# Key projection ahead of the head loop, in seven block products, with the result kept in DRAM

## What is computed

```python
x = _rmsnorm(hidden_states, ln_weight)
h_q = (x @ w_q.T).reshape(b, lq, H, DH)
h_k = (key_value_states @ w_k.T).reshape(b, lk, H, DH)
h_v = (key_value_states @ w_v.T).reshape(b, lk, H, DH)
score = jnp.einsum('bqhd,bkhd->bhqk', h_q, h_k) + position_bias[None]
# masked softmax over k
attn = jnp.einsum('bhqk,bkhd->bqhd', score, h_v).reshape(b, lq, H * DH)
return hidden_states + attn @ w_out.T
```

## Time and profile before

| what | value |
|---|---|
| median of 3 runs (lowest, highest) | 1074.19 us (1074.11, 1076.26) |
| the profiled execution, first to last instruction | 1071.4 us |
| first `turn_probs` of the loop | 73.04 us |
| last `turn_probs` but one | 903.27 us |
| busy: PE, DVE, ACT, POOL | 97%, 62%, 43%, 29% |
| bytes moved by DMA | 52.39 MB, 49 GB/s on the mean |

### The profile page before, as it was taken

The page is one execution under the profiler, slowest core; times in us unless marked ns, Lnnn a source line. Parts: engine busy times, 40 slices in busy tenths (PEclk is TensorE's granted clock), DMA queues, the critical chain, the costliest instruction groups (busy, mean ns, idle before and its releaser), DMA issues.

```text
span 1071.4 us, 16826 instructions
## 1 busy us (share of the span) xinstructions
PE 1037.1 (97%) x5946; PEld 903.5 (84%) x5946; DVE 659.0 (62%) x1189; ACT 458.9 (43%) x1090; POOL 313.4 (29%) x236
## 2 busy tenths in 40 slices
PE   8989999999999999999999999999999999799995
PEld 7778888888888888888888888888888888578784
DVE  5766666666666666666666666666666666853615
ACT  6866343434343434343434343434343434254251
POOL 1645040404040404040404040404040402343204
PEclk9999999999999999999999999999999999899998
DMA  9402020202020202020202020202020300300011
GB/s 299 134 1 84 2 84 1 83 0 83 0 83 0 83 0 83 0 83 0 83 0 83 0 83 0 83 0 83 0 83 0 122 1 20 109 21 1 1 40 40
DMA packets 20698, 52.39 MB, mean 49 GB/s; under 512 B 3136, under 2 KB 7232, under 8 KB 20672
## 3 DMA queue, kind: packets, MB, share of 16 engines
q1 hardware_dynamic: 20672, 52.06, 14.6%
HBM read 49.95 MB, written 2.10 MB: 49 GB/s over the span
## 4 chain that ended last, share of the span: by engine, by line
PE 88%; DVE 5%; POOL 2%; ACT 2%; issue 1%; DMA 1%; DVEq 0%; SPq 0%; POOLq 0%; ACTq 0%
PE psum L1330 25%; PE psum L1332 25%; PE psum L1331 25%; PE psum L1336 8%; PE psum L1337 3%; PE psum L1463 3%; DMA raw<-in_dft 1%; POOL rows L511 1%; DVE st L1045 0%; PE psum L1568 0%; DVE wts L1012 0%; POOL stat L581 0%; DVE rsum L1240 0%; ACT xn_hi L647 0%; POOL stat L583 0%
## 5 line engine op out<-in xcount | busy, mean ns | idle before, releaser
L539 POOL TENSOR_TENSOR smx<-far,bias 128x512 f32<-128x512 f32 x64 | 82.7, 1292 | 423.2 <-DVE smx L1068 421.5
L735 ACT ACTIVATE smx<-smx,nmax 128x128 f32<-128x128 f32 x256 | 99.8, 391 | 231.8 <-DVE nmax L1074 231.8
L976 DVE TENSOR_TENSOR qk<-psum,qk 128x512 fp32r<-128x512 f32 x136 | 93.2, 687 | 105.1 <-ACT qk L647 105.1
L1330 PE MATMUL psum<-wv_lo,cx_hi 128*128 128x256 f32 x512 | 149.7, 292 | 0.3 <-DVE xn_lo L976 0.3
L1332 PE MATMUL psum<-wv_hi,cx_hi 128*128 128x256 f32 x512 | 144.5, 282 | 0.0
L1331 PE MATMUL psum<-wv_hi,cx_lo 128*128 128x256 f32 x512 | 144.5, 282 | 0.0
L647 ACT ACTIVATE qk<-psum 128x512 fp32r<-128x512 f32 x136 | 80.8, 596 | 140.7 <-PE psum L1332 140.6
L976 DVE TENSOR_TENSOR vv_lo<-psum,vv_hi 128x512 fp32r<-128x512 f32 x64 | 44.2, 691 | 124.9 <-ACT vv_hi L647 124.9
L489 POOL TENSOR_TENSOR wqk_lo<-raw,wqk_hi 128x1024 fp32r<-128x1024 f32 x31 | 74.3, 2396 | 127.8 <-ACT wqk_hi L647 127.8
L1330 PE MATMUL psum<-wo_lo,at_hi 128*128 128x512 f32 x256 | 105.9, 414 | 1.1 <-issue 1.1
L1330 PE MATMUL psum<-cx_lo,wqk_hi 128*128 128x512 f32 x256 | 100.3, 392 | 1.8 <-DVE wqk_lo L976 1.8
(11 more groups left out here) (184 smaller groups left out, 2351.7 us busy)
## 6 DMA issues: line engine op xcount, KB each, us to landing
raw<-in_wqk SPq DMA_DIRECT2D x32, 512.0 KB, 3.4
raw<-in_wv SPq DMA_DIRECT2D x16, 512.0 KB, 4.3
raw<-in_wo SPq DMA_DIRECT2D x16, 512.0 KB, 3.3
raw<-in_ffn SPq DMA_DIRECT2D x10, 512.0 KB, 3.3
raw<-in_dft SPq DMA_DIRECT2D x7, 512.0 KB, 4.6
acc<-in_x SPq DMA_DIRECT2D x2, 1024.0 KB, 9.1
raw<-in_ctxT SPq DMA_DIRECT2D x4, 512.0 KB, 10.2
bias<-in_bias SPq DMA_DIRECT2D x32, 64.0 KB, 1.8
```

Of the source, the lines that this page charges most:

```text
L539: nc.gpsimd.tensor_tensor(bm, far[:, HB * hf:HB * hf + HB, :], g_, ALU.add).then_inc(s_bm_ready, 1)
L735: a.activation(exps[:, b, :], scores_sb[:, b, :], ACT.Exp, bias=nmax[:, 1, b:b + 1], accum_out=esum[:, 0, b:b + 1]).then_inc(s_exp_done, 1)
L976: return v.tensor_tensor(dst, src, hi, ALU.subtract)
L1330: mm(out, lhs(0), rhs(1), start=first, stop=False)
```

## The change

The K projection leaves the loop. All of K = context x Wk is computed ahead of the loop, pair by pair, in a phase of its own between the second Fourier transform and the first Q projection. For one pair, K is the product of a 256 x 512 matrix of weights and the 512 x 1024 context. It is cut into 2 x 2 blocks and computed by a scheme with seven block products where the plain one has eight, at the price of sums before and after: four sums of context blocks, once (T1 to T4, `t_sums` on DVE), four sums of weight blocks per pair (S1 to S4, `k_sums` and `k_last_sum` on POOL) and seven sums per pair of the products (`k_pair_dve` on DVE, with one copy by ACT, `x_copy`). A block product (`k_product`) is 6 matmuls of 512 columns; the seven of a pair go through banks 0 to 3 in turn. The four resulting blocks of a pair, 256 KB each and one for each unit j, are stored to a DRAM tensor `k_blocks` (`store_block`). In the loop they are loaded back (`load_block`) into `kf`, two to four units ahead, and split into `qk` by ACT (`k_hi`) and POOL (`k_lo`, behind `bias_and_mask`).

The loop's PE order stays, without K: Q(n+1), `turn_probs(n)`, `values(n+2)`, `attend(n)`, `scores(n+1)`, `outputs(n-2)`. `psO[1]` moves from bank 3 to `psT`, bank 2, and `turn_probs(n)` waits until `add_out` has emptied it (`s_o_add` >= 2n - 4); `values` no longer waits for `add_out`.

Also moved: the correlation of the second half (at p = 1) and its delays and norms and all transposes (at p = 5, 7, 9 and 11) go into the K phase; the weights of Q and K come as separate inputs, Q's in one piece a pair; the buffers share SBUF in another way (`av`, `wvq`, `mix`, `kf`, `ssum`, `RING` 1 for 4); the feed-forward weights take other slots, and some of them are split later (after the last unit's exponentials, one by DVE). The diff, cut to its core:

```diff
+        kd = nc.dram_tensor("k_blocks", (4 * PAIRS, P, HALF), F32, kind="Internal").ap()
...
-        psQ, psK, psT, psV = banks[0:4]
-        psO = [psK, psV]
+        psQ, psT, psV = banks[0], banks[2], banks[3]
+        psO = [banks[1], psT]
+
+        def product_bank(p, block):
+            return banks[(BLOCKS * p + block) % 4]
...
+            def store_block(p, i):
+                sp.wait_ge(s_c[i], p + 1)
+                sp.dma_start(kd[4 * p + i], staged[i]).then_inc(s_kst[i], 16)
+
+            def load_block(g, j):
+
+                if is_first(g):
+                    sp.wait_ge(s_kst[j], 16)
+                else:
+                    if isinstance(g, int):
+                        sp.wait_ge(s_k_lo, 4 * g + j - 3)
+                    else:
+                        sp.wait_ge(s_k_lo, 4 * g + (j - 3))
+                    sp.wait_ge(s_kst[j], 16 * PAIRS)
+                sp.dma_start(kf_row(j), row(kd, 4 * g + j)).then_inc(s_kf[j], 16)
...
+                    load_block(g + 1, 0)
+                    sp.wait_ge(s_wq_lo, 2 * g + 2)
+                    load_wq(g + 1)
+                    sp.wait_ge(s_wv_lo, g + 1)
+                    load_wv(g + 1)
+                    load_block(g + 1, 1)
+                load_wo(g)
+                if not last:
+                    load_block(g + 1, 2)
+                    load_bias(g + 1, 0)
+                    load_block(g + 1, 3)
+                    load_bias(g + 1, 1)
...
+            def k_sums(p):
+
+                pc = k_piece(p)
+                pool.wait_ge(s_landed[pc % SLOTS], 16 * (pc // SLOTS + 1))
+                if due(p):
+                    pool.wait_ge(s_ks_vlo, 4 * p - 2)
+                g.tensor_tensor(k_half(p, S3), k_half(p, A11), k_half(p, A21_PLACE), ALU.subtract).then_inc(s_s_sum, 1)
+                pool.wait_ge(s_s_sum, 4 * p + 1)
+                g.tensor_tensor(k_half(p, S1), k_half(p, A21_PLACE), k_half(p, A22), ALU.add).then_inc(s_s_sum, 1)
+                pool.wait_ge(s_s_sum, 4 * p + 2)
+                g.tensor_tensor(k_half(p, S2), k_half(p, S1), k_half(p, A11), ALU.subtract).then_inc(s_s_sum, 1)
+
+            def k_weights_lo(p, block, nth):
+
+                split_lo(s_ks_hi, s_ks_plo, BLOCKS * p + block + 1, k_half(p, block), k_weights(0, block),
+                         k_weights(1, block))
+
+            def k_last_sum(p):
+
+                pool.wait_ge(s_ks_plo, 3 * p + 2)
+                pool.wait_ge(s_s_sum, 4 * p + 3)
+                g.tensor_tensor(k_half(p, S4), k_half(p, A12), k_half(p, S2), ALU.subtract).then_inc(s_s_sum, 1)
+
+            def k_pair_pool(p):
+
+                if p + 1 < PAIRS:
+                    k_sums(p + 1)
+                    k_weights_lo(p + 1, A11, 1)
...
+            def k_lo(n, g_, j):
+                split_lo(s_k_hi, s_k_lo, n + 1, kf_row(j), qk[0][:, 1], qk[1][:, 1])
...
-                    if not (last and j == 3 or is_first(g) and j == 0):
+                    if not (last and j == 3):
                         bias_and_mask(n + 1, *nxt(g, j))
+                        k_lo(n + 1, *nxt(g, j))
...
+            def k_weights_hi(p, block):
+
+                if block in (A11, A12, A22):
+                    pc = k_piece(p)
+                    act.wait_ge(s_landed[pc % SLOTS], 16 * (pc // SLOTS + 1))
+                else:
+                    act.wait_ge(s_s_sum, 4 * p + {S3: 1, S1: 2, S2: 3, S4: 4}[block])
+                if p == 0:
+                    act.wait_ge(s_dft_mm, 4)
+                else:
+                    act.wait_ge(s_kp_mm, BLOCKS * (p - 1) + block + 1)
+                copy_hi(k_weights(0, block), k_half(p, block)).then_inc(s_ks_hi, 1)
+
+            def x_copy(p):
+
+                act.wait_ge(s_kp_mm, BLOCKS * p + 1)
+                if due(p):
+                    act.wait_ge(s_c[C11], p)
+                a.activation(xcopy, product_bank(p, A11), ACT.Copy).then_inc(s_xc, 1)
...
+            def k_hi(n, g, j):
+
+                act.wait_ge(s_kf[j], 16 * (g + 1))
+                if due(n):
+                    act.wait_ge(s_scores_mm, n)
+                copy_hi(qk[0][:, 1], kf_row(j)).then_inc(s_k_hi, 1)
...
+                    if front:
+                        k_hi(n + 1, *nxt(g, j))
...
+            def t_sums(c):
+
+                first, second = raw[:, (DFT_PIECES + 2 * c) % SLOTS], raw[:, (DFT_PIECES + 2 * c + 1) % SLOTS]
+                b11, b12 = first[:, 0:HALF], first[:, HALF:TOK]
+                b21, b22 = second[:, 0:HALF], second[:, HALF:TOK]
+                for i in range(2):
+                    pc = DFT_PIECES + 2 * c + i
+                    dve.wait_ge(s_landed[pc % SLOTS], 16 * (pc // SLOTS + 1))
+                if c:
+                    dve.wait_ge(s_tt_lo, 4 * c)
+                v.tensor_tensor(t_sum(T1), b12, b11, ALU.subtract).then_inc(s_t_sum, 1)
+                dve.wait_ge(s_t_sum, 4 * c + 1)
+                v.tensor_tensor(t_sum(T2), b22, t_sum(T1), ALU.subtract).then_inc(s_t_sum, 1)
+                v.tensor_tensor(t_sum(T3), b22, b12, ALU.subtract).then_inc(s_t_sum, 1)
+                dve.wait_ge(s_t_sum, 4 * c + 2)
+                v.tensor_tensor(t_sum(T4), b21, t_sum(T2), ALU.subtract).then_inc(s_t_sum, 1)
...
+            def k_pair_dve(p):
+
+                front = p + 1 < PAIRS
+                dve.wait_ge(s_xc, p + 1)
+                dve.wait_ge(s_kp_mm, BLOCKS * p + S2 + 1)
+                v.tensor_tensor(u2, product_bank(p, S2), xcopy, ALU.add).then_inc(s_tu2, 1)
...
+                dve.wait_ge(s_tu2, p + 1)
+                v.tensor_tensor(u3, product_bank(p, S3), u2, ALU.add).then_inc(s_tu3, 1)
+                if front:
...
+                dve.wait_ge(s_kp_mm, BLOCKS * p + S1 + 1)
+                dve.wait_ge(s_tu3, p + 1)
+                if due(p):
+                    dve.wait_ge(s_kst[C22], 16 * p)
+                v.tensor_tensor(staged[C22], product_bank(p, S1), u3, ALU.add).then_inc(s_c[C22], 1)
+                if due(p):
+                    dve.wait_ge(s_kst[C12], 16 * p)
+                v.tensor_tensor(staged[C12], product_bank(p, S1), u2, ALU.add).then_inc(s_tu4, 1)
...
+                dve.wait_ge(s_kp_mm, BLOCKS * p + A12 + 1)
+                if due(p):
+                    dve.wait_ge(s_kst[C11], 16 * p)
+                v.tensor_tensor(staged[C11], product_bank(p, A12), xcopy, ALU.add).then_inc(s_c[C11], 1)
+                dve.wait_ge(s_kp_mm, BLOCKS * p + A22 + 1)
+                if due(p):
+                    dve.wait_ge(s_kst[C21], 16 * p)
+                v.tensor_tensor(staged[C21], product_bank(p, A22), u3, ALU.add).then_inc(s_c[C21], 1)
+                if p == 2:
+                    top(7)
+                if p in (6, 8, 10, 12):
+                    xt_lo(p - 6)
+                    xt_lo(p - 5)
+                dve.wait_ge(s_kp_mm, BLOCKS * p + S4 + 1)
+                dve.wait_ge(s_tu4, p + 1)
+                v.tensor_tensor(staged[C12], product_bank(p, S4), staged[C12], ALU.add).then_inc(s_c[C12], 1)
+                if front:
+                    k_weights_lo(p + 1, S4)
...
+            def k_product(p, block):
+
+                if block in (A11, A12, A22):
+                    pe.wait_ge(s_ks_plo, 3 * p + {A11: 1, A12: 2, A22: 3}[block])
+                else:
+                    pe.wait_ge(s_ks_vlo, 4 * p + {S2: 1, S3: 2, S1: 3, S4: 4}[block])
+                if p == 0 and block == A11:
+                    pe.wait_ge(s_cx_lo, CTX_PIECES)
+                    pe.wait_ge(s_tt_lo, 8)
+                if p == 0 and block in (A11, S2, S3, S1):
+                    pe.wait_ge(s_sq_lo, 4 + block + 1)
+                elif block == A11:
+                    pe.wait_ge(s_tu4, p)
+                elif block == S2:
+                    pe.wait_ge(s_c[C11], p)
+                elif block == S3:
+                    pe.wait_ge(s_c[C21], p)
+                elif block == S1:
+                    pe.wait_ge(s_c[C12], p)
+                elif block == A12:
+                    pe.wait_ge(s_xc, p + 1)
+                elif block == A22:
+                    pe.wait_ge(s_tu2, p + 1)
+                else:
+                    pe.wait_ge(s_tu3, p + 1)
+
+                def rows_of(i, c):
+                    if block in T_OF_BLOCK:
+                        return t_rows(i, T_OF_BLOCK[block], c)
+                    if block == S4:
+                        return cx[i][:, 2 + c, HALF:TOK]
+                    return cx[i][:, (2 if block == A12 else 0) + c, 0:HALF]
+
+                for c in range(2):
+                    last = mm3(product_bank(p, block)[:, :], lambda i: k_weights(i, block)[:, c * P:(c + 1) * P],
+                               lambda i: rows_of(i, c), c == 0, c == 1)
+                last.then_inc(s_kp_mm, 1)
+
+            def k_pair_pe(p):
+                for block in range(BLOCKS):
+                    k_product(p, block)
...
                 if due(n):
                     pe.wait_ge(s_t_lo, n)
-                if isinstance(n, int) and n < 2:
```

(90 more changed lines are left out.)

770 lines of the change are left out of this document (420 added, 350 removed).

## The result

The changed kernel takes 1186.7 us (1186.44 to 1194.42, 4 runs), the kernel before 1075.13 beside it: a ratio of 1.106, 95% interval 1.103 to 1.110. It is slower by 112 us; 1178 was forecast, with a range of 1135 to 1225. The profiled execution has a span of 1184.6.

What follows compares the result with a forecast made beforehand. PE bounds the kernel, with the chain attend, softmax, turn close under it. Loop start 234.4, first two steps 10.3 and 12.1, sixty steps 740.4, clock 10, rest 168.1 and 2.8 give 1178 us, range 1135 to 1225.

Steps and rivals of the forecast that it cites:

- The step's two bounds: Loop step: PE work falls to 10.65 us, but the chain attend, softmax, turn sets 12.22, or 12.71 at j = 1.
- The last link: End of the loop's chain: turn_probs waits for the second add_out, behind softmax_out on DVE, to empty its bank.
- the rival that the bank is free earlier: Wait before turn_probs: the bank change does not bind, step 11.6, 42 us less, 1136; chance 0.08.
- K's split on POOL: Loop: k_lo on POOL, about 1.2 to 1.3 us, ends some 4 before scores; costs nothing, bounds 0 to 0.5 a step.
- The rival that it would hold the multiplication: Loop: POOL's k_lo starts before the softmax multiplication L1086 and holds it, 1.2 us a step, 1250; chance 0.05.
- The loop's start: First turn_probs, after products and the work between: at 234.4 us, where the kernel before has 73.04.
- the wait ahead of the products: Before the first block product: DVE and POOL sums and splits exclude one another, start at 51 us; 41 if side by side.
- The products: K phase ahead of the loop: 152.5 us of block products on PE, plus 5.7 corr, 3 transposes, 4.5 stalls and clock.
- the rival of another engine: K phase: another engine than PE leads the products, a pair takes 12 instead of 9.5, 40 us more, 1218; chance 0.10.
- The clock: Loop: some half of the fifteen steps with a gap of 2.06 us lose the clock, + 10 us, bounds 0 and 24.
- The rival of a fall in each step: Loop: the clock falls after the 1.57 us gaps too, 96 us instead of 10, total 1264; chance 0.10.
- The rest: Everything from turn_probs(62) to the end: taken unchanged at 168.1 us, within 5 either way.

Runs made afterwards that it cites:

- best_b: Changed kernel with scores ahead of attend, second-half squares earlier, context low parts on DVE, second output bank back at values' bank; 1055.8 us, ratio 0.984 to the kernel before.
- add_first: Changed kernel with both DVE additions of outputs(n-2) ahead of the softmax's last part; 1142.8 us, ratio 1.063 to the kernel before.
- bank_back: Changed kernel with the second output bank back at values' bank 3, so values waits for the addition and turn_probs does not; 1153.0 us, ratio 1.073.
- scores_tuned: Changed kernel with scores ahead of attend; on DVE softmax_in before V's split, both additions before softmax_out, attend's low part after it; 1083.6 us, ratio 1.007.
- squares_first: Changed kernel with ACT squaring the second half before copying mirrored lags, and DVE splitting those squares before the four maxima; 1187.0 us, ratio 1.104.
- wv_late: Changed kernel with ACT copying the Wv piece behind, not ahead of, the copy of attend's result in j = 1 steps; 1198.2 us, ratio 1.115.
- scores_first: Changed kernel with scores(n+1) ahead of attend(n) on PE, and softmax_in(n+1) ahead of the low part of attend's result on DVE; 1072.2 us, ratio 0.998.

## Why the prediction was right, step by step

**The step's two bounds** held. PE's work without K was put at 10.65; best_b's steps are 10.66. The chain was put at 12.22 and 12.71; the steps are 12.28 and 12.78. `attend` to the end of the addition is 8.86 in both (424.66 to 433.52), PE's reaction 0.06 in both; the 0.07 that is missing lies between `turn_probs` and `attend`, 3.37 for 3.30, since `values` starts 0.41 behind a `turn_probs` that has waited (421.70 behind 421.29) and 0.35 behind the one of the earlier trace rows that has not (502.22 behind 501.87). Over sixty steps the step was put 3.8 us too low, the largest error that stays in the sum.

**The last link**, the bank of `turn_probs`, was read rightly from the order of DVE's instructions in the trace of before, where no wait of PE ended on that addition. add_first and bank_back show it. The price of the rival that the bank is free earlier does not come out of the sum's own terms: 60 x 0.60 is 36, not 42, and the falls' 10 would go with it. Freed, it was worth 34 in bank_back and 44 in add_first.

**K's split on POOL** at no cost: right, and by the margin named, an order of start. The rival that it would hold the multiplication came true in scores_tuned, where it started 0.06 sooner.

**The loop's start**, 234.4, is 234.54, but this is not as good as it looks. The step that failed is the wait ahead of the products. I had the first product wait for the sums and splits, DVE and POOL in turn, to 51. They did exclude one another, and were done at 45.16; what PE waited for was the split of the squares behind four maxima, which I had counted nowhere: I took what the first product reads, and not what its banks still held. The two errors, 6 us too much and 5 us too little, nearly cancel in 49.86. squares_first shows the cause of the start; it also shows that the order saved little, as the maxima have to be done anyway before the count that follows the first pair.

**The products** took 216.98 - 49.86 = 167.1 where 165.7 was forecast, a pair of seven between two groups of transposes 9.57 (19.14 for two) where 9.5 was forecast. PE led: from 50 to 217 its waits add up to 1.9, and the rival of another engine falls. Between products and loop lie 17.6 (17.7 forecast).

**The clock**: 10 forecast, with some half of the fifteen j = 1 gaps in mind; nine falls of 1.49 make 13.4. The gaps were read rightly: 1.57 and 2.06 count from where the next matmul would have started, the profile's idle time from the modelled end of the last one, 0.16 later, and there they are 1.40 and 1.90. The rival of a fall in each step fails. The Trainium skill, TensorE: Matmul & The Clock Gate, section HAM oscillation — how this bites in real kernels, shows a loop that waits in each iteration for longer than it works, and starts each one cold. Here PE worked for 10.7 and was idle for 1.4 to 1.9 in a step, so that example was no ground for the 1264, and nine steps of sixty had a fall. That some half of the fifteen would fall was a guess: the prediction gives no ground for the half, and why nine fell and six did not stays open.

**The rest** behind `turn_probs` 62 took 169.8 for 168.1. With 0.4 up to `turn_probs` 2, 3.8 in the steps, 3.4 by the clock and 1.7 here the span is 9.3 over the forecast 1175.3; the median lies 2.1 above the span instead of 2.8.

## What to carry to other kernels

Before work is taken off the engine that is busy for 97%, time the dependent chain that closes the loop in one step of the trace: if it is nearly as long as the step, the work taken out turns into waiting, unless the order changes with it. Here the same arithmetic cost 10.6% in the old order and gained 1.6% on the kernel before with `scores` ahead of `attend`, an earlier start and the bank where it was. The kernel before was not run in the new order; PE never stops in its steps, so there the order alone had nothing to gain in them. When a buffer moves to another bank, look for the last instruction that frees it, and where that stands in its engine's order.

## What the runs showed of the hardware

DVE and POOL hold one another up by whole instructions, and a start of 0.06 or 0.14 sooner decides which one pays (1.78 for 0.69 on DVE, or 1.70 for 1.29 on POOL). It reaches an operation on four elements with one source. The earlier trace rows had this already (L1074, 2.29), but the expectations of wv_late and scores_tuned gave it no price or left it to a rival: L1299 took 1.18 beside POOL in wv_late and 0.66 in the j = 1 steps of scores_first and best_b (L1295 there), while the reduction L1297, with one source of 512, kept 0.69. The Trainium skill, SBUF — State Buffer, section Who interferes with whom, lists `tensor_scalar` among the operations that can take the ports shared with GpSimd and `tensor_reduce` among those that don't on this chip, and says that the order of issue decides who blocks; the trace agrees, with these numbers.

The clock fell behind idle times of 1.90 in eight of fourteen steps of the changed kernel, and behind 2.40 (wv_late) in ten of fourteen; behind 1.60 and less it stayed at 2.4 GHz in all of the sixty steps of these kernels. The length of the idle time alone does not decide: the falls behind 1.90 come in threes, with two j = 2 steps without one in between. In the changed kernel they are at units 18, 22, 26 and 38, 42, 46; in squares_first, with the same gaps and a start 0.9 sooner, at 26, 30, 34 and 46, 50, 54. Behind the 2.3 us ahead of unit 2 the clock fell in scores_tuned (a step of 12.45) and stayed in scores_first (10.87). This points to the moment at which the idle time comes; what sets it was not tried.
